# A gated transformer block on one core: SiLU products of batch 1 on VectorE, a fused variance, and another hand-set order

## The chip, the cores and the metric

The kernel runs on one core of a Trainium2 chip. The metric is the device time of one execution in microseconds, as the median of several runs. The profile is one execution; its times count from the first instruction.

## The reference

Four batches (B = 4) of 256 tokens with 128 features pass four sublayers, each with a residual scaled by the tanh of a gate:

```
x = x + tanh(g_xattn[0]) * L0_xattn(layernorm(x), ctx)      # autocorrelation attention over Fourier transforms, 16 heads
x = x + tanh(g_ffn[0])   * L0_ffn(layernorm(x))             # product-key memory, 8 heads, top 8 of 32 x 32 keys
x = x + tanh(g_xattn[1]) * L1_xattn(layernorm(x), ctx)      # attention with rotary positions, 16 heads of 8
x = x + tanh(g_ffn[1])   * L1_ffn(layernorm(x))             # 8 experts of 336 hidden units
```

In the product-key memory the queries `q = x @ w_q` (2048 columns) are normalised by their mean and variance over all tokens before they meet the keys:

```
mean, var = jnp.mean(q, axis=(0, 1)), jnp.var(q, axis=(0, 1))
q = (q - mean) * rsqrt(var + 1e-5) * gamma + beta
sim = einsum('pbnhd,hkpd->pbnhk', q, keys)        # then top 8 of each half, top 8 of the sums, softmax
h = softmax(scores) * gelu(x @ down_embed[indices]); out = h @ up_embed[indices]
```

Every expert of the last sublayer computes `y = (silu(x @ gate_w[e].T) * (x @ up_w[e].T)) @ down_w[e].T`, and the outputs are added with the router's probabilities, those past a token's own number of experts set to zero.

## The kernel before

Everything is float32 apart from one-hot and gathered operands in float16. The first sublayer, the layer norm behind it and the similarities run for all batches together, in the order of the code, up to about 96 us. **The variance** of the 2048 query columns comes from the covariance of the normalised input: TensorE makes `w_q.T @ cov` for 16 groups of 128 columns into six PSUM banks (`CW_BANK`), three groups a bank. VectorE copies the mean column, multiplies the bank by `w_qT` (L904) and, after a wait on its own product, sums it per column (L905). From the variance come the scaled keys `keyS` (L914), from them TensorE's product `M`, and from M the similarities (`similar`), tile by tile. Products with all down embeddings (`down_all`, 16 of them, for the GELU on ScalarE) are put in between; `EARLY` says how many of the first four ScalarE takes ahead of M, and three of them stand on TensorE ahead of M.

From there on each engine runs **a list of named steps written out by hand**, `ORDER` ("pe", "act", "dve", "pool"), a step being a name, a batch and a number: `gate2.7` is the eighth gate product of batch 2. An engine never passes a step whose semaphores are not yet there. Steps of the later text, in the order of one batch:

- retrieval: `best`, `where` (index search, L936), `pair`, `weight` (softmax and expert numbers, first line L978), `number`, `onehots`, `groups`, then for eight pieces of 32 tokens `place` (L1035, one-hot), `token` (TensorE), `half` and `weigh` (L1047, L1052), and `mix`, TensorE's product with the up embeddings; `norms1` adds it to x (L1060) and starts the next layer norm, whose root is on GpSimd (L439 to L446)
- attention: `turn_2`, `query`, `rope`, `turn_q`, four `by_query` with a maximum `max` each (L1097), `neg_max` (L1435 on TensorE), `score`, `prob`, `value`, `keep`, `out_turn`, `attend`, `project` (the product with Wo), `norms3` (again L1060 and GpSimd's root), `turn_3` (L1515)
- experts: 21 steps `gate` a batch, each 128 hidden units with the gate half and the up half in one of two PSUM banks; `silu` (L694), `times`, and for each expert a `down` on TensorE and a `gather` on VectorE (L1155, L1157), `moe_out` at the end; `route1`, `route2` and `rank` make the router's scores.

For batches outside `DIRECT`, ScalarE copies the up half to SBUF besides the SiLU, which frees the bank, and GpSimd multiplies the two (L433). For batches in `DIRECT` (2 and 3) VectorE multiplies the SiLU by the up half in PSUM (L1167), and that frees the bank: `gate` waits for it.

```
pe.wait_ge(sem("av_ready" if (m - 2) // NB in DIRECT else "gate_ready"), m - 1)
```

Of the kernel before, what the change touches and what calls it, by code (L numbers as in the profile page):

```python
# [66 lines left out]
gate0.2 by_query1.2 route20.0 token2.3 gate0.3 gate0.4 by_query1.3 token2.4 gate0.5 gate0.6 neg_max1.0 token2.5
gate0.7 score1.0 down0.0 token2.6 score1.1 value1.0 token2.7 score1.2 value1.1 mix2.0 score1.3 down0.1 onehots3.0
value1.2 gate0.8 gate0.9 value1.3 gate0.10 down0.2 turn_22.0 gate0.11 query2.0 gate0.12 out_turn1.0 turn_q2.0 token3.0
by_query2.0 down0.3 gate0.13 by_query2.1 attend1.0 token3.1 gate0.14 by_query2.2 gate0.15 token3.2 gate0.16 down0.4  # L70
by_query2.3 gate0.17 token3.3 gate0.18 project1.0 neg_max2.0 gate0.19 down0.5 token3.4 gate0.20 score2.0 down0.6
token3.5 turn_31.0 score2.1 value2.0 token3.6 gate1.0 score2.2 token3.7 route11.0 gate1.1 mix3.0 value2.1 gate1.2
route21.0 gate1.3 score2.3 down0.7 turn_23.0 gate1.4 value2.2 query3.0 gate1.5 down1.0 gate1.6 value2.3 gate1.7
turn_q3.0 down1.1 by_query3.0 gate1.8 out_turn2.0 gate1.9 by_query3.1 gate1.10 down1.2 gate1.11 down1.3 gate1.12
attend2.0 by_query3.2 gate1.13 project2.0 gate1.14 by_query3.3 gate1.15 down1.4 gate1.16 neg_max3.0 gate1.17 turn_32.0
gate1.18 gate1.19 score3.0 down1.5 gate1.20 down1.6 gate2.0 route12.0 gate2.1 route22.0 score3.1 down1.7 gate2.2
# [48 lines left out]
addb1.0 times0.11 times0.12 times0.13 times0.14 times0.15 times0.16 norms31.0 times0.17 times0.18 times0.19 times0.20  # L125
times1.0 times1.1 norms13.0 times1.2 times1.3 times1.4 times1.5 times1.6 addb2.0 times1.7 times1.8 times1.9 times1.10
times1.11 times1.12 times1.13 norms32.0 times1.14 times1.15 times1.16 times1.17 times1.18 addb3.0 times1.19 times1.20
norms33.0
# [1514 lines left out]
```

## Time and profile before

| quantity | value |
|---|---|
| median of 3 runs | 458.83 us (458.66 to 462.54) |
| the profiled execution's own time | 460.18 us |
| its span, first to last instruction | 458.3 us |
| mean granted TensorE clock | 0.881 |
| TensorE busy | 384.7 us (84%) |
| VectorE busy | 331.0 us (72%) |
| ScalarE busy | 197.4 us (43%) |
| GpSimd busy | 105.8 us (23%) |

Shares are averages over stages with different limits, so they say where to look and not what binds. The granted clock is the share of full speed that TensorE was given.

### The profile page before, as it was taken

How to read it: one execution, taken by the hardware profiler on the slowest of the kernel's cores; microseconds unless marked ns; L12 is line 12 of the kernel's file. 1: busy time of each engine (PE TensorE's matmuls, PEld its weight loads, DVE VectorE, ACT ScalarE, POOL GpSimd, SP SyncE). 2: the span in 40 equal slices, each digit the busy share in tenths (PEclk: the TensorE clock that was granted, in tenths of full speed). 3: DMA queues.
4: the chain of work that ended last, by engine and by line, in shares of the span. 5: the costliest groups of instructions: out<-in, count | busy, mean ns of one | idle time of the engine just before them, and what ended most of it. 6: DMA issues, size and time to landing. Idle time of an engine off the chain costs nothing.

```text
span 458.3 us, 8058 instructions
## 1 busy us (share of the span) xinstructions
PE 384.7 (84%) x2848; PEld 296.5 (65%) x2848; DVE 331.0 (72%) x1235; ACT 197.4 (43%) x399; POOL 105.8 (23%) x221
## 2 busy tenths in 40 slices
PE   8977699943462588995998899989999999999896
PEld 3856665412451366773787678866788886787785
DVE  7987674999999999989999888942444434354533
ACT  2453442551121011542486852366832698527221
POOL 2000020305047430073032381160432610010000
PEclk9989897985565575799599999988999999999999
DMA  7950000040000000000000000000000000000000
GB/s 228 332 224 0 1 1 2 1 153 8 1 1 1 1 1 0 1 2 1 1 2 1 1 2 2 0 1 2 12 2 0 1 1 14 1 0 1 13 0 11
DMA packets 5772, 11.80 MB, mean 26 GB/s; under 512 B 2020, under 2 KB 4325, under 8 KB 5222
## 3 DMA queue, kind: packets, MB, share of 16 engines
q1 hardware_dynamic: 5734, 11.31, 7.0%
q8 instruction: 22, 0.36, 0.3%
q14 instruction: 16, 0.13, 0.1%
HBM read 10.78 MB, written 0.52 MB: 25 GB/s over the span
## 4 chain that ended last, share of the span: by engine, by line
PE 37%; DVE 32%; issue 3%; ACT 3%; POOL 1%; DVEq 0%; ACTq 0%
PE ps L1193 35%; DVE mx L1097 5%; DVE Xb L1035 4%; DVE HDb L1052 3%; DVE tix L936 2%; DVE top L929 2%; DVE Y L1027 2%; PE ps L1435 1%; DVE pk L945 1%; DVE Xb L1047 1%; DVE xnb L1157 1%; ACT L564 1%; DVE Sb L1047 1%; DVE sb_downT L1017 1%; DVE hot L984 1%
## 5 line engine op out<-in xcount | busy, mean ns | idle before, releaser
L1193 PEld LDWEIGHTS ps<-dnb,Sb 128*128 128x128 f32 x448 | 54.2, 193 | 9.3 <-issue 3.9
L1193 PE MATMUL ps<-dnb,Sb 128*128 128x128 f32 x448 | 56.9, 279 | 3.8 <-POOL Sb L433 2.3
L1193 PE MATMUL ps<-Y,Xb 128*128 128x32 f16 x512 | 39.9, 250 | 15.8 <-DVE Xb L1035 10.6
L1193 PEld LDWEIGHTS ps<-Y,Xb 128*128 128x128 f16 x512 | 37.3, 162 | 23.1 <-DVE Xb L1035 17.1
L694 ACT ACTIVATE Sb<-ps 128x256 f32<-128x256 f32 x84 | 31.8, 382 | 37.4 <-PE ps L1193 37.4
L1157 DVE SCALAR_TENSOR_TENSOR xnb<-ps,score,xnb 128x128 f32<-128x128 f32 x56 | 17.0, 346 | 40.3 <-PE ps L1193 40.2
L1193 PE MATMUL ps<-ctxTb,sb_guT 128*128 128x256 f32 x168 | 45.5, 401 | 0.1
L1193 PE MATMUL ps<-Xb,sb_guT 128*128 128x256 f32 x168 | 43.7, 391 | 1.8 <-DVE Sb L1167 1.2
L471 ACT ACTIVATE Sb<-ps 128x256 f32<-128x256 f32 (+2 forms) x54 | 26.2, 492 | 35.8 <-PE ps L1193 20.0
L433 POOL TENSOR_TENSOR Sb<-Sb 128x256 f32<-128x256 f32 x28 | 21.7, 781 | 85.8 <-ACT Sb L694 85.8
L564 ACT ACT_TABLE_LOAD x32 | 41.1, 1283 | 0.6
L1035 DVE TENSOR_TENSOR Xb<-sb_downT,iox 128x2048 f16<-128x2048 f16 x32 | 39.6, 1248 | 1.7 <-PE ps L1193 1.3
L1097 DVE TENSOR_REDUCE mx<-ps 128x8 f32<-128x2048 f32 x16 | 36.6, 2286 | 3.8 <-PE ps L1193 3.7
L1167 DVE TENSOR_TENSOR Sb<-Sb,ps 128x256 f32<-128x256 f32 x42 | 17.4, 420 | 26.5 <-ACT Sb L694 26.2
L651 ACT ACTIVATE probs<-ps 128x1024 f32<-128x1024 f32 x32 | 31.2, 1020 | 9.2 <-PE ps L1193 9.1
L1193 PEld LDWEIGHTS ps<-Xb,sb_guT 128*128 128x128 f32 x168 | 29.1, 190 | 9.4 <-DVE Sb L1167 3.9
L1193 PEld LDWEIGHTS ps<-ctxTb,sb_guT 128*128 128x128 f32 x168 | 30.2, 197 | 7.3 <-issue 3.0
L1193 PE MATMUL ps<-KTb,Sb 32*128 32x256 f32 x256 | 21.3, 453 | 3.7 <-DVE mx L1097 3.5
L1193 PE MATMUL ps<-sb_upl,HDb 128*128 128x128 f32 x128 | 17.9, 306 | 4.6 <-DVE HDb L1052 4.6
L1193 PEld LDWEIGHTS ps<-sb_upl,HDb 128*128 128x128 f32 x128 | 17.1, 219 | 6.1 <-DVE HDb L1052 6.1
L936 DVE FIND_INDEX8 tix<-top,simb 128x8 uint32<-128x32 f32 x128 | 20.8, 185 | 0.0
L1193 PE MATMUL ps<-Sb,KTb 32*128 32x256 f32 x256 | 20.2, 434 | 0.1
(278 smaller groups left out, 707.0 us busy)
## 6 DMA issues: line engine op xcount, KB each, us to landing
sb_guT<-in_guT SPq DMA_DIRECT2D x1, 2688.0 KB
dnb<-in_dn SPq DMA_DIRECT2D x1, 1792.0 KB
simb<-in_w_q SPq DMA_DIRECT2D x1, 1024.0 KB, 4.9
simb<-in_w_qT SPq DMA_DIRECT2D x1, 1024.0 KB, 7.0
Gb<-in_ctx SPq DMA_DIRECT2D x1, 512.0 KB, 3.7
Gb<-in_dft SPq DMA_DIRECT2D x1, 512.0 KB, 4.5
sb_x<-in_x SPq DMA_DIRECT2D x1, 512.0 KB
sb_downT<-in_downT SPq DMA_DIRECT2D x1, 512.0 KB, 8.0
```

What stands on the lines that cost most here:

```text
L433: g.tensor_tensor(av[:, m % 6, :], av[:, m % 6, :], up[m % 3], ALU.mult).then_inc(sem("av_ready"), 1)
L471: act.activation(dst, src, ACT.Copy, scale=scale).then_inc(sem(s), 1)
L564: act.activation(sm[:, 63:64], tg[:, 0:1], func).then_inc(sem("table_ready"), 1)
L651: act.activation(probs[:, g % 2, 2 * half:2 * half + 2, :], ps[:, 4 + 2 * half:6 + 2 * half, :], ACT.Exp, scale=float(1.0 / np.sqrt(DK))). ...
L694: act.activation(av[:, m % 6, :], ps[:, m % 2, 0:256], ACT.Silu).then_inc(sem("gate_ready"), 1)
L936: i = v.max_index(tix[:, q, g, :], top[:, q, g, :], s3[:, g, :])
L1035: v.tensor_tensor(X[:, c % 2, :, :].rearrange("p (c e) t -> p c e t", c=EH), elS[:, :, c * TC:c * TC + TC].unsqueeze(2).broadcast_to([P, E ...
L1052: v.tensor_tensor(HD.rearrange("p e (s t) -> p s e t", s=2)[:, :, :, c * TC:c * TC + TC], w[:, :, :].rearrange("p s (t e) -> p s e t", e=E ...
L1097: v.tensor_reduce(mx[:, :, 4 * g:4 * g + 4].rearrange("p t r -> p r t"), ps[:, 4:8, :].rearrange("p r (t k) -> p r t k", t=2), AX, ALU.max)\
L1157: i = v.scalar_tensor_tensor(macc[:, t, :], y, w, macc[:, t, :], ALU.mult, ALU.add)
L1167: v.tensor_tensor(av[:, m % 6, :], av[:, m % 6, :], ps[:, m % 2, 256:512], ALU.mult).then_inc(sem("av_ready"), 1)
L1193: return pe.matmul(o, l, r, start=start, stop=stop)
```

## The change

Four things change. (1) The product and the sum of the variance become one fused instruction per group of 128 columns, with the sum as an accumulated output: 16 instructions instead of 6 products and 6 sums. (2) `EARLY` is 2 instead of 4: one `down_all` stands ahead of M instead of three, and the other three of the first four follow the first four `similar`; ScalarE takes their GELUs in the same order. (3) `DIRECT` gains batch 1: its 21 products leave GpSimd for VectorE, the 21 copies on ScalarE go, and its gates wait for VectorE's product. (4) All four lists of `ORDER` are written anew; batch 0 keeps its products on GpSimd.

```diff
@@ ORDER
-onehots0.0 token0.0 token0.1 token0.2 token0.3 token0.4 token0.5 token0.6 token0.7 mix0.0 onehots1.0 warm0.0 turn_20.0
...
+onehots0.0 token0.0 token0.1 token0.2 token0.3 token0.4 token0.5 token0.6 token0.7 mix0.0 onehots1.0 turn_20.0
...
@@ -305,9 +306,9 @@
             return 5 if b == 0 and c % 2 else 3
 
         G_BANK = [4 + n % 4 for n in range(2 * EH)]
-        EARLY = 4
+        EARLY = 2
         WARM = 3
-        DIRECT = (2, 3)
+        DIRECT = (1,2,3)
 
         block = ctx.enter_context(nc.Block())
 
@@ -588,8 +589,9 @@
             copy(M[:, :], ps[:, 7, :], "M_ready")
             similar(2)
             similar(3)
-            gelu(EARLY - 1)
-            for n in range(EARLY, EH):
+            for n in range(EARLY - 1, 4):
+                gelu(n)
+            for n in range(4, EH):
                 similar(n)
                 gelu(n)
             soft(0, 0)
@@ -901,8 +903,9 @@
                 cw = ps[:, bank, 0:m * (D + 1)].rearrange("p (c d) -> p c d", d=D + 1)
                 w = tmp[:, c0 * D:(c0 + m) * D].rearrange("p (c d) -> p c d", d=D)
                 v.tensor_copy(var[:, 2, c0:c0 + m], cw[:, :, D])
-                link(v.tensor_tensor(w, cw[:, :, 0:D], ld["w_qT"][:, c0:c0 + m, :], ALU.mult))
-                i = v.tensor_reduce(var[:, 3, c0:c0 + m], w, AX, ALU.add)
+                for c in range(m):
+                    i = v.scalar_tensor_tensor(w[:, c, :], cw[:, c, 0:D], 1.0, ld["w_qT"][:, c0 + c, :], ALU.mult, ALU.mult,
+                                               accum_out=var[:, 3, c0 + c:c0 + c + 1])
                 i.then_inc(sem("cw_used"), 1)
             v.wait_ge(sem("cw_used"), len(CW_BANK))
             link(v.tensor_tensor(var[:, 2, :], var[:, 2, :], var[:, 2, :], ALU.mult))
@@ -1342,7 +1345,7 @@
             for t in range(4):
                 shifted(t)
             pe.wait_ge(sem("xn1T_ready"), 1)
-            for n in range(3):
+            for n in range(EARLY - 1):
                 down_all(n)
             for c in range(16):
                 if c % 8 == 0:
@@ -1353,7 +1356,8 @@
             pe.wait_ge(sem("xcT_ready"), 1)
             for t in range(4):
                 similar(t)
-            down_all(3)
+            for n in range(EARLY - 1, 4):
+                down_all(n)
             for t in range(4, NT):
                 shifted(t)
                 similar(t)
```

**VectorE, before `norms3` of batch 0** (its three rows are the last of each list; L1108 and L1111 are the attention's divisions, sb_x is x). Before:

```order
L1108 RECIPROCAL rcp<-ps 128x32
L1109 TENSOR_TENSOR xnb<-ps,rcp 128x256
L1009 SCALAR_TENSOR_TENSOR whl<-ps,whl 128x128
L1014 TENSOR_TENSOR Xb<-elT,iox 128x1024
L1017 TENSOR_TENSOR sb_downT<-elT,sb_io 128x1024
L1027 TENSOR_TENSOR Y<-Xb,whl 64x1024 x4
L1060 SCALAR_TENSOR_TENSOR sb_x<-ps,tg,sb_x 128x256
L1065 BN_STATS st<-sb_x 128x6 x2
L1068 BN_AGGR mv<-st 128x2 x2
```

After (Xb is the one-hot of `place`, L788 to L793 the rope):

```order
L1111 RECIPROCAL rcp<-ps 128x32
L1112 TENSOR_TENSOR xnb<-ps,rcp 128x256
L1038 TENSOR_TENSOR Xb<-sb_downT,iox 128x2048 x2
L1095 MEMSET Sb 128x32
L788 TENSOR_TENSOR Sb<-ps,cs 128x256
L789 TENSOR_TENSOR Sb<-ps,cs 128x256
L792 TENSOR_TENSOR Sb<-Sb 128x32x4
L793 TENSOR_TENSOR Sb<-Sb 128x32x4
L1063 SCALAR_TENSOR_TENSOR sb_x<-ps,tg,sb_x 128x256
L1068 BN_STATS st<-sb_x 128x6 x2
L1071 BN_AGGR mv<-st 128x2 x2
```

Two `place` and the rope of batch 1 now stand between the divisions and `norms3`. Further up in the list the same holds of an index search, a `weight` and a `pair` of batch 3, ahead of that block:

```order
L939 MAX_INDEX tix<-top,simb 128x8 x16
L981 TENSOR_TENSOR hot<-pkf,iox 128x1280
L985 TENSOR_TENSOR hot<-hot,candi 128x1280
L987 TENSOR_TENSOR hot<-hot 128x640
L987 TENSOR_TENSOR hot<-hot 128x320
L988 TENSOR_REDUCE eid<-hot 128x64
L993 TENSOR_REDUCE zz<-ex_ 128x8
L994 RECIPROCAL zz<-zz 128x8
L995 TENSOR_TENSOR wts<-ex_,zz 128x8x8
L1063 SCALAR_TENSOR_TENSOR sb_x<-ps,tg,sb_x 128x256
L1068 BN_STATS st<-sb_x 128x6 x2
L1071 BN_AGGR mv<-st 128x2 x2
```

These are `where3.1` and `weight3.0`, and behind them `norms1` of batch 1; before, `where3.0` stood there directly in front of it.

**TensorE, from `project1.0` (sb_Wo) to `down0.6` (dnb, the last row).** Before:

```order
L1193 MATMUL ps<-sb_Wo,ctxTb 128x128 x2
L1435 MATMUL ps<-sb_ident,Sb 128x128 x8
L1193 MATMUL ps<-ctxTb,sb_guT 128x256 x2
L1193 MATMUL ps<-dnb,Sb 128x128 x6
L1193 MATMUL ps<-Y,Xb 128x2x16 x16
L1193 MATMUL ps<-ctxTb,sb_guT 128x256 x2
L1193 MATMUL ps<-Sb,KTb 128x256 x8
L1193 MATMUL ps<-dnb,Sb 128x128 x8
```

After:

```order
L1196 MATMUL ps<-sb_Wo,ctxTb 128x128 x2
L1196 MATMUL ps<-KTb,Sb 128x256 x8
L1196 MATMUL ps<-Y,Xb 128x2x16 x16
L1196 MATMUL ps<-dnb,Sb 128x128 x6
L1196 MATMUL ps<-ctxTb,sb_guT 128x256 x2
L1439 MATMUL ps<-sb_ident,Sb 128x128 x8
L1196 MATMUL ps<-Y,Xb 128x2x16 x16
L1196 MATMUL ps<-Sb,KTb 128x256 x8
L1196 MATMUL ps<-dnb,Sb 128x128 x8
```

A `by_query` (KTb) and a `token` (Y,Xb) have moved behind `project1.0`, and a `gate` (sb_guT) that stood ahead of `down0.6` stands behind it.

**VectorE among the first maxima of batch 3 (L1100; L1170 is the product with the up half, L1160 a `gather`).** After:

```order
L1158 TENSOR_SCALAR xnb<-ps,score 128x128 x2
L1170 TENSOR_TENSOR Sb<-Sb,ps 128x256
L1160 SCALAR_TENSOR_TENSOR xnb<-ps,score,xnb 128x128 x2
L1170 TENSOR_TENSOR Sb<-Sb,ps 128x256
L1100 TENSOR_REDUCE mx<-ps 128x4x2
L1160 SCALAR_TENSOR_TENSOR xnb<-ps,score,xnb 128x128 x2
L1170 TENSOR_TENSOR Sb<-Sb,ps 128x256 x3
L1100 TENSOR_REDUCE mx<-ps 128x4x2
L1170 TENSOR_TENSOR Sb<-Sb,ps 128x256
L1160 SCALAR_TENSOR_TENSOR xnb<-ps,score,xnb 128x128 x2
```

Before, these products were not on VectorE: between the maxima stood `gather` steps and the attention's divisions alone.

## Rows read from the trace of the kernel before

**Rows 1.** Stretches: busy us (instructions) of PE, PEld, DVE, ACT, POOL, clock, DMA, GB/s.
```profile
100.00:262.00 162.00, 114.77 (x1019) 90.03 (x1020) 154.09 (x624) 54.89 (x108) 51.51 (x119) 0.73 0.03 10
...
312.00:458.00 146.00, 138.37 (x1044) 112.67 (x1040) 62.86 (x183) 76.92 (x162) 22.76 (x47) 1.00 0.02 5
...
407.00:458.00 51.00, 45.09 (x280) 38.55 (x278) 22.42 (x71) 17.14 (x39) 1.53 (x6) 1.00 0.02 6
```

**Rows 2.** Timeline, 294 to 305 us: start, us, engine, instruction, [idle before, releaser].
```profile
294.64 0.61 PE L1193 MATMUL ps<-sb_Wo,ctxTb 128*128 128x128 f32 x4
...
297.68 0.23 POOL L439 TENSOR_SCALAR rs<-mv 128x2 f32<-128x2 f32 x1 [5.77 <-DVE mv L1068]
...
299.61 1.12 POOL L444 TENSOR_SCALAR rs<-rs 128x2 f32<-128x2 f32 x1
...
304.11 1.16 PE L1193 MATMUL ps<-dnb,Sb 128*128 128x128 f32 x8 [2.28 <-POOL Sb L433]
```

**Rows 3.** Stretches of 4 us behind that wait.
```profile
306.00:310.00 4.00, 4.00 (x38) 2.95 (x36) 2.36 (x5) 2.25 (x4) 0.00 (x0) 0.50 0.00 0
310.00:314.00 4.00, 4.00 (x40) 2.34 (x36) 0.71 (x2) 2.64 (x4) 0.00 (x0) 0.71 0.01 2
```

**Rows 4.** Timeline of VectorE in the variance, 54 to 70 us.
```profile
61.57 0.15 DVE L903 COPY var<-ps 128x3 f32<-128x3 f32 x1
...
62.69 0.15 DVE L903 COPY var<-ps 128x3 f32<-128x3 f32 x1
...
64.92 0.17 DVE L742 TENSOR_SCALAR var<-var 128x16 f32<-128x16 f32 x1
```

**Rows 5.** Timeline at 262 us, and the groups by form (busy us, mean ns).
```profile
262.72 0.61 DVE L1157 SCALAR_TENSOR_TENSOR xnb<-ps,score,xnb 128x128 f32<-128x128 f32 x2 [1.54 <-PE ps L1193]
...
L936 DVE MATCH_VALUE_LOAD tix<-top,simb 128x8 f32 x128 | 9.3, 72 | 0.1
```

**Rows 6.** Stretches of 1 us in M, TensorE alone: busy (matmuls), clock.
```profile
69.00:70.00 1.00, 1.00 (x11) 0.99 0.00 0
70.00:71.00 1.00, 1.00 (x7) 0.50 0.00 0
```

**Rows 7.** The chain that ended last: an index search of 16 pieces.
```profile
129.40 2.58 DVE tix L936 x16
```

**Rows 8.** Timeline, 247 to 263 us.
```profile
247.53 1.25 PE L1193 MATMUL ps<-Y,Xb 128*128 128x32 f16 x16 [1.16 <-DVE Sb L1047]
...
255.65 0.81 DVE L978 TENSOR_TENSOR hot<-pkf,iox 128x1280 f16<-128x1280 f16 x1
255.79 3.84 PE L1193 MATMUL ps<-sb_upl,HDb 128*128 128x128 f32 x32 [1.57 <-DVE HDb L1052]
...
259.90 0.48 DVE L1060 SCALAR_TENSOR_TENSOR sb_x<-ps,tg,sb_x 128x256 f32<-128x256 f32 x1
...
262.52 0.27 PE L1380 MATMUL ps<-sb_ident,elh 128*128 128x128 f32 x1
```

**Rows 9.** Groups of the page: busy us, mean ns, idle time before them.
```profile
L433 POOL TENSOR_TENSOR Sb<-Sb 128x256 f32<-128x256 f32 x28 | 21.7, 781 | 85.8 <-ACT Sb L694 85.8
...
L1035 DVE TENSOR_TENSOR Xb<-sb_downT,iox 128x2048 f16<-128x2048 f16 x32 | 39.6, 1248 | 1.7 <-PE ps L1193 1.3
L1097 DVE TENSOR_REDUCE mx<-ps 128x8 f32<-128x2048 f32 x16 | 36.6, 2286 | 3.8 <-PE ps L1193 3.7
L1167 DVE TENSOR_TENSOR Sb<-Sb,ps 128x256 f32<-128x256 f32 x42 | 17.4, 420 | 26.5 <-ACT Sb L694 26.2
```

**Rows 10.** Timeline, 203 to 221 us.
```profile
203.26 0.48 DVE L1060 SCALAR_TENSOR_TENSOR sb_x<-ps,tg,sb_x 128x256 f32<-128x256 f32 x1 [1.35 <-PE ps L1193]
...
212.62 0.48 DVE L1060 SCALAR_TENSOR_TENSOR sb_x<-ps,tg,sb_x 128x256 f32<-128x256 f32 x1
...
216.72 0.88 ACT L627 ACTIVATE xnb<-sb_x,nb,rs 128x128 f32<-128x128 f32 x2 [6.33 <-POOL nb L446]
...
220.55 0.66 PE L1515 MATMUL ps<-sb_ident,xnb 128*128 128x128 f32 x2
```

More of the change, by code:

```diff
@@ L67 @@
[L67 to L76, printed above, removed]
@@ new lines @@
+score1.0 down0.0 token2.5 score1.1 value1.0 token2.6 down0.1 token2.7 value1.1 score1.2 mix2.0 score1.3 down0.2
+onehots3.0 value1.2 gate0.8 gate0.9 value1.3 gate0.10 out_turn1.0 turn_22.0 gate0.11 query2.0 down0.3 gate0.12
+turn_q2.0 token3.0 gate0.13 by_query2.0 gate0.14 token3.1 attend1.0 gate0.15 by_query2.1 gate0.16 down0.4 by_query2.2
+gate0.17 token3.2 gate0.18 project1.0 by_query2.3 token3.3 down0.5 gate0.19 neg_max2.0 token3.4 score2.0 down0.6
+token3.5 gate0.20 score2.1 turn_31.0 token3.6 route11.0 gate1.0 token3.7 gate1.1 gate1.2 mix3.0 gate1.3 down0.7
@@ L107 @@
-pair3.0 attend0.0 groups2.0 norms30.0 where3.1 rope1.0 place2.0 pair3.1 place2.1 weigh2.0 place2.2 max1.0 place2.3
-weigh2.1 max1.1 place2.4 weigh2.2 max1.2 route20.0 weigh2.3 place2.5 max1.3 neg_max1.0 weigh2.4 rank0.0 place2.6
-weigh2.5 place2.7 gather0.0 weigh2.6 weight3.0 weigh2.7 weight3.1 norms12.0 gather0.1 groups3.0 gather0.2 place3.0
-rope2.0 place3.1 attend1.0 place3.2 max2.0 gather0.3 weigh3.0 max2.1 weigh3.1 place3.3 max2.2 weigh3.2 gather0.4
-place3.4 max2.3 neg_max2.0 weigh3.3 norms31.0 gather0.5 place3.5 weigh3.4 place3.6 gather0.6 weigh3.5 place3.7
@@ new lines @@
+weigh0.7 best2.0 weight1.1 where2.0 norms10.0 best2.1 groups1.0 where2.1 place1.0 pair2.0 rope0.0 place1.1 weight2.0
+weigh1.0 max0.0 place1.2 place1.3 weigh1.1 max0.1 weigh1.2 pair2.1 max0.2 place1.4 weigh1.3 max0.3 place1.5 neg_max0.0
+weigh1.4 place1.6 weight2.1 weigh1.5 place1.7 best3.0 weigh1.6 where3.0 best3.1 pair3.0 weigh1.7 where3.1 weight3.0
+norms11.0 pair3.1 groups2.0 attend0.0 place2.0 place2.1 rope1.0 norms30.0 weight3.1 place2.2 weigh2.0 max1.0 weigh2.1
+max1.1 place2.3 max1.2 weigh2.2 place2.4 max1.3 route20.0 neg_max1.0 weigh2.3 rank0.0 place2.5 weigh2.4 place2.6
@@ new lines @@
+gather0.0 weigh2.5 place2.7 weigh2.6 gather0.1 weigh2.7 norms12.0 gather0.2 groups3.0 attend1.0 place3.0 place3.1
+rope2.0 place3.2 gather0.3 weigh3.0 max2.0 weigh3.1 max2.1 place3.3 gather0.4 max2.2 weigh3.2 place3.4 norms31.0
+max2.3 neg_max2.0 weigh3.3 gather0.5 place3.5 weigh3.4 place3.6 gather0.6 place3.7 weigh3.5 weigh3.6 times1.0 weigh3.7
+times1.1 times1.2 norms13.0 gather0.7 times1.3 moe_out0.0 route21.0 rank1.0 times1.4 times1.5 rope3.0 gather1.0
+times1.6 gather1.1 times1.7 max3.0 gather1.2 times1.8 times1.9 times1.10 max3.1 times1.11 gather1.3 times1.12
@@ L124 @@
-times0.2 times0.3 times0.4 times0.5 look_a3.1 times0.6 number3.0 norms12.0 times0.7 times0.8 times0.9 times0.10
[L125 to L128, printed above, removed]
+look_a0.1 look_a1.0 cands1.0 cands1.1 gap1.0 look_a1.1 gap1.1 number1.0 look_a2.0 cands2.0 norms10.0 addb0.0 cands2.1
@@ L129 @@
+look_a2.1 gap2.0 gap2.1 cands3.0 number2.0 cands3.1 gap3.0 look_a3.0 look_a3.1 gap3.1 norms11.0 norms30.0 times0.0
+times0.1 times0.2 times0.3 times0.4 times0.5 times0.6 times0.7 number3.0 norms12.0 times0.8 times0.9 times0.10
+times0.11 times0.12 times0.13 times0.14 times0.15 times0.16 addb1.0 norms31.0 times0.17 times0.18 times0.19 addb2.0
+times0.20 norms13.0 norms32.0 addb3.0 norms33.0
 """,
```

81 lines of the change are left out of this document (41 added, 40 removed).

## The prediction

> **What bounds the kernel now.** I read the stretches first, then who waits for whom, then the timeline at the waits. The stretches [rows 1] give two regimes. From 100 to 262 us VectorE is busy 154.1 of 162 us: it does the key retrieval of all four batches and the attention maxima, and TensorE, busy 114.8 us at 0.73 of its clock, fits in between. Later TensorE is the bound: from 312 us on it is busy 138.4 of 146 us. So a VectorE microsecond taken away before 262 counts, one after it counts only if TensorE stands behind it; and behind 262 only TensorE's gaps and its half clock can be won. The largest such gap is one of 2.28 us at 301.8 us, where `down` of batch 0 waits for a multiplication on GpSimd; after it the clock reads 0.50 (1.2 GHz) for some microseconds [rows 2, 3]. Behind the last matmul a fixed tail of 3.4 us follows.
>
> **Part 1, the variance (58 to 71 us).** VectorE is on the path: TensorE waits for the scaled keys with which this work ends, and makes the product M from them. A group of three columns takes 1.12 us now, from one copy to the next (61.57 to 62.69) [rows 4]; the six take 5 x 1.12 + 0.7 = 6.3 us. The change makes three fused instructions per group, 16 in all, without the wait between product and sum. Its nearest row is a fused multiply-add from PSUM over 128x128: two of them take 0.61 us, so one starts some 0.27 us behind the other [rows 5]. No row has an accumulated output. If writing out the sum is free, a group costs 0.07 + 3 x 0.27 = 0.88 and all six 4.7 us (1.6 less); if it costs as much as a 16-element instruction, 0.17 [rows 4], a group costs 1.39 and all six 7.4 us (1.1 more). I take 0.07, the mean of the smallest instruction here, the value load of the index search [rows 5]: 1.09 a group, 5.8 us, 0.5 less. The Trainium skill (VectorE: DVE Perf Modes, section "Two Vector instructions with no wait between them") says that such an operation is two instructions, the main one and a read of the accumulator; it gives no time for the second, and no row here has one.
>
> With it goes EARLY 4 to 2: two `down_all` matmul pairs, 0.86 us each, are no longer ahead of M but behind the first four `similar`. In the trace they hide nothing that is missed: M starts on the keys (VectorE), and the GELUs have slack to 112 us. But TensorE now stands idle about 1.4 us before M, and its clock fell to 0.50 during M's narrow matmuls already (70 to 76 us), when it did 7 instead of 11 of them in a microsecond [rows 6]. Should it fall two microseconds sooner, M is about 1 us longer; if all of M runs so, 4.3 us become 6.7 (2.4 more). I take 0.5 more. Together part 1 is worth **0**, with ends at -1.6 and +2.4 (less of the one cancels the other).
>
> **Part 2, the new order up to the third mix (100 to 262 us).** VectorE's work is the same in total up to batch 2's residual, plus one `gather` of 0.61 us; it is in another sequence. Ahead of `norms3` of batch 0, the step that opens the mixture of experts, now stand `where3.1`, `weight3.0`, `pair3.1`, `place2.0`, `place2.1` and `rope1.0`: 2.6 + 4.2 + 2.0 + 2.5 + 1.2 = 12.5 us by their like in the trace: an index search of 16 pieces 2.58; a weight step from 255.65 to the next step's start at 259.90; a pair, with eight searches instead of sixteen and eight maxima, estimated at 2.0; 1.25 for each `place`; and a rope of four products, estimated from the 0.42 of a product of such a size [rows 7 to 9]. An idle spot goes, since something independent now stands in front of it: 1.35 us before the residual of batch 1; and some 0.3 of a smaller one before its divisions, in all 1.7 [rows 10]. So `norms3` starts at 212.6 + 12.5 - 1.7 = 223.4 us, and by the same 5.1 us through GpSimd and ScalarE the turn on TensorE (220.55 now, its input ready at 217.6) at 228.5: 8.0 us later [rows 10]. TensorE may not start a gate before it.
>
> Not all of this is lost, since in the stretch that follows VectorE has less left. Ahead of `weigh2.7` stand only `weight3.1` (4.1) and `gather0.1` (0.6) more than now, 4.7 us, less the 1.7: by VectorE the third `mix` starts 3.0 us later, at 258.8 instead of 255.79. By TensorE: from the turn to the mix it takes 35.2 us now, with 1.16 and 1.57 us of waits for VectorE [rows 8]; these go, `by_query1.0` (1.1) has moved ahead and `down0.1` (1.6) comes in: 33.0 us, so 261.5. The later one decides; with what remains of the half clock I take 261.1, which is +5.3 us. Against it stands `down0.1`, done already (1.6), and the transposition behind `down0.2`, which now waits for GpSimd's numbers until 262.5 and has them early then (0.5) [rows 8]. **+3.2**, ends +0.9 (VectorE alone decides) and +6.
>
> **Part 3, the gap at 301.8 us.** `project1.0` ends at 295.25; the residual and its statistics follow on VectorE, GpSimd's root from 297.68 to some 301.6, and only then the two multiplications that `down0.6` wants: TensorE goes on at 304.11 after 2.28 us [rows 2]. The clock is then 0.50 and 0.71 in two stretches of 4 us, 2.0 + 1.2 = 3.2 us of work [rows 3]. In the new order GpSimd's queue is the same at this place, `norms31` ahead of `times0.17`; the batch 1 multiplications that leave it stood behind. But TensorE has `by_query2.3` and `token3.3` between `project1.0` and `down0.6` and has lost `gate0.20`: 1.1 us each, so about 1.1 to 1.5 us more cover. The wait shrinks to about 0.8 us, the waits of 1.16 and 1.57 us before 247.53 and 255.79 us were followed by no such clock, and I count the half clock as won: **-4.8**. If all stays it is 0, if all goes -5.6.
>
> **Part 4, 21 multiplications to VectorE.** GpSimd loses 21 of some 0.78 us, ScalarE 21 copies, about 8 us if they cost what an activation of that size does, VectorE gains 21 of 0.42 us (8.8 us) [rows 9]; it is busy 62.9 of 146 us from 312 us on, so the work itself is covered. ScalarE's 8 us are not on the path either: only at 380 to 392 us does TensorE wait there. What is new is a wait: `gate1.n` on TensorE now needs the multiplication two before it, and that stands in VectorE's queue behind maxima of 2.29 us [rows 9], four of them, and the ranking, which I estimate at 3.5 us from its sixteen small steps of 0.17 to 0.3. Everything in TensorE's order queues behind the gate. The fourth batch has this wait on all its gates: TensorE is busy 45.1 of 51 us, and 3.4 of the rest are the tail, so 2.5 us for a batch, with a VectorE that has no maxima left [rows 1]. In the new order a `down`, `score` or `by_query` step stands between most pairs of gates. I take **+1.0**, ends 0 and +5.6 (one maximum and one ranking exposed).
>
> **Sum.** 0 + 3.2 - 4.8 + 1.0 = -0.6 us. The profiled run has a span of 458.3 us and a time of 460.18; the median of the runs shown is 458.83, and 1% (4.6 us) is about what a measurement of this kernel can tell from no change. I set the difference against the median: **458.2 us**, no change, its own range 454.5 to 462.5.
>
> **Rivals.** *Slower: VectorE's queue rules batch 1.* If the free steps between a gate and the multiplication it wants cover only about 1 us, each of four maxima shows 1.3 us and the ranking 2.3: 7.5 instead of 1.0, 464.7 us. For it: four maxima, the ranking and the rope lie among `times1.4` to `times1.17`. Against: VectorE is half idle there, and between the third maximum and the gate that follows TensorE has `down` and `value` steps of 1 to 2 us. It decides from about 2 us of exposed queue in half of the places.
> *Faster: VectorE alone decides at the mix.* Then the third mix starts at 258.8 (2.3 less), the gap at 301.8 goes whole (0.8), nothing is lost in batch 1 (1.0), and ScalarE without the copies shortens the waits of 380 to 392 us (1.2): 452.9 us. For it: the steps moved ahead fill real gaps. Against: TensorE has no slack from the turn on.
> *The gap stays.* A root of eight small GpSimd operations took 4.0 us from 297.68 on, one of them 1.12, while VectorE ran `place`; the one before 216.72, without it, took under 3 [rows 2, 10]; if it is held up as long again, 0.8 becomes 2.3 with the half clock: 463.0 us. The Trainium skill (GPSIMD Engine Reference, "1. Specifications") says that GpSimd's SBUF interfaces are shared with VectorE, in contention with its two-port modes and with two SBUF inputs; by that rule, the trace agrees, and such a hold would come wherever `place` stands beside the root.
> *The fused variance brings nothing* (accumulator read 0.17): +1.6 on any case.
>
> **Chances.** Forecast 0.38, faster rival 0.28, slower 0.22, gap stays 0.12. 452.9 with its spread lies mostly, the forecast's low end partly under 454.2: faster 0.31; 464.7 mostly and 463.0 for a third above 463.4, with the forecast's high end 0.25; same 0.44. The range takes in the middles of both outer rivals: 451 to 465.5.
>
> **What would show it.** The variance: six groups in less than 6.3 us. Part 2: the first gate at 228 to 230 us, the third mix at 259 to 262. Part 3: no GpSimd wait over 1 us in front of `down0.6` and a clock of 1.00 behind it. Part 4: TensorE's waits for the multiplication line sum to under 4 us in batch 1. I would be wrong if the maxima wait for TensorE in a chain (VectorE idle over 10 us before 262 us), which none of these terms has.

## The result

The changed kernel takes **462.67 us** (median of 8 runs, 462.31 to 464.07); the kernel before takes 458.63 us beside it (8 runs). The ratio is 1.0068, 95% interval [1.0038, 1.0098]: 0.7% slower, small and outside the measurement's uncertainty. The forecast was 458.2. In a later session the same comparison gave 1.0051 [1.0016, 1.0087]. The profiled execution has a span of 461.5 us, a time of 463.25 and a granted clock of 0.885.

I take the steps in the order of time. **The variance**, as VectorE's timeline shows it (start, us, instruction):

```profile
57.43 0.16 DVE L905 COPY var<-ps 128x3 f32<-128x3 f32 x1 [4.32 <-PE ps L1196]
57.51 0.28 DVE L907 SCALAR_TENSOR_TENSOR Gb<-ps,simb 128x128 f32<-128x128 f32 x1
57.71 0.08 DVE L907 DVE_READ_ACCUMULATOR Gb<-ps,simb 128x1 f32 x1
57.71 0.29 DVE L907 SCALAR_TENSOR_TENSOR Gb<-ps,simb 128x128 f32<-128x128 f32 x1
...
58.13 0.16 DVE L905 COPY var<-ps 128x3 f32<-128x3 f32 x1
...
63.33 0.76 DVE L917 TENSOR_TENSOR Gb<-Gb,var 128x256 f32<-128x256 f32 x2
...
70.42 0.69 DVE L922 COPY simb<-ps 128x512 f32<-128x512 f32 x1 [6.33 <-PE ps L1196]
```

A group of three takes 58.13 - 57.43 = 0.70 us, where it was 1.12 [rows 4]: fused instructions start 0.20 to 0.21 us apart, and the accumulator's read is a record of its own of 0.08 us that lies under the next one. The keys are scaled 5.90 us behind the first copy (8.30 before), and the first similarities leave PSUM 12.99 us behind it (15.91 before). I count from the first copy, since its own place varies from 57.4 to 60.6 us between the profiled executions, whatever the kernel.

**The turn of batch 0 into the experts.** The timeline from 209 us on, where GpSimd, ScalarE, TensorE and VectorE hand over to one another:

```profile
209.72 2.00 POOL L414 TENSOR_TENSOR dd<-sc 128x64 f32<-128x64 f32 x1 [4.03 <-DVE pk L948]
...
211.67 0.95 POOL L417 CAST pkf<-pk 128x64 f16<-128x64 uint32 x1
212.35 0.72 POOL L440 TENSOR_SCALAR rs<-mv 128x2 f32<-128x2 f32 x1
...
217.91 0.20 POOL L447 TENSOR_TENSOR nb<-rs 128x2 f32<-128x2 f32 x1
218.14 0.88 ACT L629 ACTIVATE xnb<-sb_x,nb,rs 128x128 f32<-128x128 f32 x2 [9.14 <-POOL nb L447]
219.07 0.69 PE L1422 MATMUL ps<-sb_ident,xnb 128*128 128x128 f32 x2 [7.98 <-ACT xnb L629]
...
223.34 0.39 DVE L788 TENSOR_TENSOR Sb<-ps,cs 128x256 f32<-128x256 f32 x1 [5.84 <-issue]
...
224.50 0.48 DVE L1063 SCALAR_TENSOR_TENSOR sb_x<-ps,tg,sb_x 128x256 f32<-128x256 f32 x1
...
231.87 0.33 PE L1519 MATMUL ps<-sb_ident,xnb 128*128 128x128 f32 x1 [1.29 <-ACT xnb L629]
```

L414 and L417 are `gap3.1`; L440 to L447 are the root of batch 1's layer norm (`norms11.0`), L1422 its turn, L788 the rope that needs this batch's queries, L1063 `norms3` of batch 0 and L1519 its turn. The statistics of that layer norm were there at about 207.7 us; the root begins at 212.35, because GpSimd stands at `gap3.1`, whose input comes from VectorE's `pair3.1`. TensorE then waits 7.98 us, VectorE 5.84 us in front of the rope. The turn is at 231.87, where it was 220.55 [rows 10].

**Behind the turn.** The stretches of the page's columns (PE, PEld, DVE, ACT, POOL busy, clock), and TensorE's timeline:

```profile
100.00:232.00 132.00, 76.83 (x653) 60.59 (x654) 122.01 (x540) 26.17 (x53) 50.24 (x107) 0.65 0.01 5
...
306.00:310.00 4.00, 3.93 (x49) 3.43 (x47) 3.93 (x7) 3.69 (x7) 3.47 (x4) 1.00 0.02 4
310.00:314.00 4.00, 4.00 (x48) 3.26 (x47) 3.69 (x6) 2.48 (x4) 0.00 (x0) 1.00 0.00 0
```

```profile
265.00 1.27 PE L1196 MATMUL ps<-sb_upl,HDb 128*128 128x128 f32 x9
...
428.66 1.13 PE L1196 MATMUL ps<-Xb,sb_guT 128*128 128x256 f32 x4 [1.21 <-DVE Sb L1170]
...
456.24 1.58 PE L1196 MATMUL ps<-dnb,Sb 128*128 128x128 f32 x12 [0.79 <-DVE xnb L1160]
```

The third `mix` starts at 265.00 without a wait (255.79 and 1.57 us of wait before [rows 8]). From its start to the end of the last matmul, 457.82, it is 192.8 us; before it was 198.9. The wait for GpSimd at `down0.6` is gone, and so is the half clock behind it (0.50 and 0.71 in [rows 3], 1.00 now). So the change gains in the variance and in the tail, and loses more in between: from 100 to 262 us VectorE stands idle for 14.9 us, where it was 7.9.

### The profile page after: what moved, and what is told of

The parts are those of the page before. It is cut to its first block, busy times and chain, and to the rows that moved or that the text cites. A ratio compares the mean times of both kernels' runs of the same rounds, so it can differ in the third digit from the quotient of the medians.

```text
span 461.5 us, 8058 instructions
## 1 busy us (share of the span) xinstructions
PE 378.7 (82%) x2848; PEld 293.9 (64%) x2848; DVE 334.8 (73%) x1276; ACT 192.9 (42%) x378; POOL 95.5 (21%) x200
## 4 chain that ended last, share of the span: by engine, by line
PE 40%; DVE 5%; ACT 4%; issue 3%; POOL 1%; DVEq 0%; ACTq 0%
PE ps L1196 38%; ACT L565 2%; PE ps L1439 1%; ACT probs L653 1%; DVE Xb L1038 1%; DVE Sb L1170 1%; ACT Sb L696 1%; DVE Y L1030 1%; DVE mx L1100 0%; POOL Sb L434 0%; DVE xnb L1160 0%; ACT Sb L472 0%; POOL nb L447 0%; PE ps L1519 0%; DVE sb_downT L1020 0%
## 5 line engine op out<-in xcount | busy, mean ns | idle before, releaser
L1170 DVE TENSOR_TENSOR Sb<-Sb,ps 128x256 f32<-128x256 f32 x63 | 25.9, 419 | 39.0 <-ACT Sb L696 37.0
L1100 DVE TENSOR_REDUCE mx<-ps 128x8 f32<-128x2048 f32 x16 | 36.6, 2286 | 3.0 <-PE ps L1196 2.8
L1196 PEld LDWEIGHTS ps<-Xb,sb_guT 128*128 128x128 f32 x168 | 29.1, 190 | 10.2 <-DVE Sb L1170 6.2
L472 ACT ACTIVATE Sb<-ps 128x256 f32<-128x256 f32 (+2 forms) x40 | 21.1, 534 | 31.1 <-PE ps L1196 18.0
L1160 DVE SCALAR_TENSOR_TENSOR xnb<-ps,score,xnb 128x128 f32<-128x128 f32 x56 | 17.0, 345 | 21.2 <-PE ps L1196 21.1
L440 POOL TENSOR_SCALAR rs<-mv 128x2 f32<-128x2 f32 x8 | 2.9, 358 | 100.1 <-DVE mv L1071 100.1
L1196 PE MATMUL ps<-KTb,Sb 32*128 32x256 f32 x256 | 19.0, 412 | 2.8 <-DVE mx L1100 2.8
```

The source lines that it names most:

```text
L472: act.activation(dst, src, ACT.Copy, scale=scale).then_inc(sem(s), 1)
L1100: v.tensor_reduce(mx[:, :, 4 * g:4 * g + 4].rearrange("p t r -> p r t"), ps[:, 4:8, :].rearrange("p r (t k) -> p r t k", t=2), AX, ALU.max)\
L1160: i = v.scalar_tensor_tensor(macc[:, t, :], y, w, macc[:, t, :], ALU.mult, ALU.add)
L1170: v.tensor_tensor(av[:, m % 6, :], av[:, m % 6, :], ps[:, m % 2, 256:512], ALU.mult).then_inc(sem("av_ready"), 1)
L1196: return pe.matmul(o, l, r, start=start, stop=stop)
```

## The experiments

First all of them in one table. "Copy to similar" is from VectorE's first variance copy to its first copy of the similarities, "to mix 2" to TensorE's second `mix`, "to the turn" to the turn of batch 0 (L1519 of the changed kernel), "to the end" to the end of the last matmul; all in us, of the profiled execution.

| run | median, us | ratio to before, 95% | copy to similar | to mix 2 | to the turn | to the end |
|---|---|---|---|---|---|---|
| before | 458.63 | | 15.9 | 141.2 | 162.3 | 396.4 |
| after | 462.67 | 1.0068 [1.0038, 1.0098] | 13.0 | 142.7 | 174.4 | 400.4 |
| changed_again | 462.65 | 1.0051 [1.0016, 1.0087] | 13.1 | 142.6 | 174.4 | 400.3 |
| root_first | 456.60 | 0.9947 [0.9911, 0.9984] | 12.4 | 140.7 | 168.0 | 392.9 |
| norms30_first | 457.80 | 0.9956 [0.9932, 0.9980] | 12.7 | 142.4 | 170.3 | 393.8 |
| direct_off | 460.30 | 0.9990 [0.9952, 1.0028] | 12.4 | 140.6 | 167.9 | 396.7 |
| part1 | 457.16 | 0.9955 [0.9921, 0.9990] | 12.5 | 138.1 | 159.3 | 390.8 |
| fused_only | 457.83 | 0.9966 [0.9930, 1.0003] | 15.5 | 141.2 | 162.4 | 393.8 |
| early_only | 460.42 | 0.9978 [0.9939, 1.0017] | 18.2 | 145.1 | 166.3 | 397.3 |
| early_again, one run | 457.13 | | 15.4 | 140.9 | 162.0 | 393.5 |
| head_before | 457.61 | 0.9956 [0.9921, 0.9991] | 12.4 | 138.6 | 159.9 | 392.7 |
| part1_times | 459.51 | 0.9964 [0.9923, 1.0004] | 12.4 | 138.8 | 160.0 | 397.8 |
| part1_times_again, one run | 459.55 | | 13.1 | 138.1 | 159.3 | 395.8 |

The kernel before had medians of 459.31 (root_first, part1, fused_only, head_before), 460.15 (direct_off, part1_times, early_only, changed_again) and 459.95 us (the rest) in the three later sessions, so ratios are compared, not medians across sessions. The column "to mix 2" is there because after, changed_again, root_first, norms30_first and direct_off have the same steps on every engine up to that point, so what differs there is not their edit.

### root_first: the root ahead of gap3.1

```diff
@@ ORDER "pool" of the changed kernel
-look_a3.1 gap3.1 norms11.0 norms30.0
+look_a3.1 norms11.0 gap3.1 norms30.0
```

> The changed kernel with one pair swapped in GpSimd's list: norms11.0 (the root of batch 1's layer norm) ahead of gap3.1 instead of behind it. In the changed kernel the root starts at 212.35 us, 4.7 us after its input, because gap3.1 waits for a VectorE step that comes later, and VectorE then stands idle for 5.84 us before the rope of batch 1. Theory (GpSimd's queue delays the front): the root runs from about 207.8 us, the idle before the rope falls from 5.84 to under 2 us, the turn of batch 0 on TensorE comes 3 to 5 us earlier than 231.87, and as TensorE is busy without a gap from there, the time falls by 3 to 5 us, to 457.5 to 459.5. Rival (the VectorE steps moved ahead of norms3 delay it, and the idle only shifts): less than 1 us, 461.5 to 462.7.

Its timeline at the same place:

```profile
206.53 0.22 POOL L440 TENSOR_SCALAR rs<-mv 128x2 f32<-128x2 f32 x1 [2.07 <-DVE mv L1071]
...
208.49 1.88 POOL L445 TENSOR_SCALAR rs<-rs 128x2 f32<-128x2 f32 x1
...
211.17 0.62 POOL L447 TENSOR_TENSOR nb<-rs 128x2 f32<-128x2 f32 x1
211.75 0.29 POOL L414 TENSOR_TENSOR dd<-sc 128x64 f32<-128x64 f32 x1
...
212.76 0.69 PE L1422 MATMUL ps<-sb_ident,xnb 128*128 128x128 f32 x2 [2.91 <-ACT xnb L629]
...
217.61 0.39 DVE L788 TENSOR_TENSOR Sb<-ps,cs 128x256 f32<-128x256 f32 x1 [1.21 <-issue]
...
226.14 0.44 PE L1519 MATMUL ps<-sb_ident,xnb 128*128 128x128 f32 x2 [1.01 <-ACT xnb L629]
```

The idle time ahead of the rope falls from 5.84 to 1.21 us, the turn comes 6.5 us earlier behind the first copy, and the kernel is 1.2 points faster than the changed one (0.9947 against 1.0068; the two intervals do not meet). Of the 6.5 us, 2.0 are there at the second `mix` already, ahead of the moved step, and are not its doing (TensorE's clock behind M, below). Counted from the second mix, the turn comes 4.5 us earlier and the last matmul 5.5 (the clock from the turn to the third mix reads 0.95 here and 0.90 there). One word in the list of the least busy engine was worth some 5 us. **changed_again** rules out that the chip made it:

> The changed kernel once more, unchanged, in the same session as the others, since the sessions differ by up to 1 us. Theory: 0.5 to 1% above the kernel before, 5 to 7 us above root_first's 456.6; the root of batch 1's layer norm starts 4 to 6 us later than in root_first, after a gap3.1 operation of about 2 us. Rival (the chip of the first session made the difference, not GpSimd's order): within 2 us of root_first's distance to the kernel before.

It gave 1.0051 and the same distances within 0.2 us. The first theory held.

### part1, fused_only, early_only, early_again: the variance taken apart

All four keep the order and the GpSimd products of the kernel before. part1 has the fused variance and `EARLY = 2`, fused_only the fused variance with `EARLY = 4`, early_only the old product and sum with `EARLY = 2`; early_again is early_only once more.

```diff
-        EARLY = 4
+        EARLY = 2          # part1, early_only, early_again
-                link(v.tensor_tensor(w, cw[:, :, 0:D], ...))     # part1, fused_only
-                i = v.tensor_reduce(var[:, 3, c0:c0 + m], w, AX, ALU.add)
+                    i = v.scalar_tensor_tensor(w[:, c, :], ..., accum_out=var[:, 3, c0 + c:c0 + c + 1])
```

> The kernel before with the fused variance and EARLY = 2 alone: its own order, batch 1 on GpSimd. In the changed kernel the first similarity tile was copied 3.7 us earlier (70.42 against 74.11). Theory (VectorE is the bound up to 262 us, so it passes on): 3.0 to 3.8 us faster than before, 454.9 to 455.7. Rival (M and the clock took it by chance in one execution, or it is lost in a wait of the retrieval): less than 1.5 us faster, 457.2 to 458.7. If the prediction's sizes held (0.5 for the fused step, nothing for EARLY): 458.1.

> The kernel before with the fused variance alone, EARLY = 4 as before. Between the first copy and the scaled keys the changed kernel took 5.90 us against 8.30, 2.4 less. If the fused step alone makes the gain: 2.4 us faster than before and within 0.5 of the run with both. If EARLY = 2 holds the clock up during M or frees the start of M: up to 1.3 us less of a gain than that run. With EARLY = 4 two more matmul pairs of 0.86 us stand ahead of M, and the keys now come 2.4 us sooner, so M should wait for these matmuls: I expect 1.0 to 2.0 us less gain than with both, that is 0.7 to 2.4 us faster than before.

> The kernel before with EARLY 2 instead of 4 and the variance in its two old steps. Theory (the fused variance and EARLY work together: with EARLY 4 the fused one only waits, with EARLY 2 alone the keys are still late): from the first variance copy to the first copy of sim 15.0 to 15.9 us, against 15.9 before, 15.5 with the fused variance alone and 12.5 with both; time within 1 us of the kernel before. Rival (EARLY alone does it, because the two pairs held M back and let the clock fall): 13.5 us or less and 2 us or more faster than before.

> early_only a second time, one look, since one profile can't tell whether the half clock in M belongs to the kernel. Theory (M behind an idle spot of 1.7 us falls to half clock): M's 32 narrow matmuls and their two copies take 6.5 us or more again, granted clock 0.50 from 68 us on, first variance copy to first copy of sim 17.5 us or more. Rival (chance of one execution): clock 1.00 in M, 15 to 16 us.

From first copy to similarities, against 15.9 before: both parts 12.5, the fused variance alone 15.5, `EARLY` alone 15.4 (early_again). So neither does much alone and both together 3.4 us. By the medians the three can't be told apart: 0.9955 with both, 0.9966 and 0.9978 with one, intervals overlapping. So part1, 2.1 us faster than the kernel before by its ratio, falls between its two expectations, and fused_only, 1.6 us faster, inside its own. TensorE's timeline in fused_only shows one half of the reason:

```profile
63.46 2.74 PE L1195 MATMUL ps<-dnb,sb_downT 128*128 128x512 f32 x6
66.03 1.20 PE L1195 MATMUL ps<-Gb,simb 128*128 128x32 f32 x10
```

The keys are ready at about 64 us, and M starts at 66.03, behind six matmuls (`down_all`), of which `EARLY = 2` leaves two. With `EARLY = 2` and the old variance it is the other way round: TensorE is free and the keys come late. So M starts 8.6 and 8.8 us behind the first copy with one part, 8.8 before, and 6.9 with both (part1, root_first). My prediction looked at the two edits one at a time, and the profile of before already had the warning:

```profile
64.27 2.74 PE L1193 MATMUL ps<-dnb,sb_downT 128*128 128x512 f32 x6
```

These six matmuls end as M starts (66.98), so earlier keys alone had next to nothing to win.

The other half is the clock behind M. Stretches of TensorE (busy, matmuls, clock) in fused_only, and then in root_first:

```profile
70.00:72.00 2.00, 1.31 (x3) 0.50 0.00 0
72.00:74.00 2.00, 2.00 (x4) 0.50 0.00 0
```

```profile
70.00:72.00 2.00, 2.00 (x6) 1.00 0.00 0
72.00:74.00 2.00, 2.00 (x6) 1.00 0.03 8
```

All four profiles that lack one or both parts read 0.50 from M's last matmuls on (early_only from its first), for some 6.8 us in three of them, the kernel before among them, and 10.2 in early_only. Of the nine profiles with both parts, five read it for some 3.4 us (after, changed_again, norms30_first, part1, part1_times_again) and four not at all (root_first, direct_off, head_before, part1_times). So in these profiles the two edits together shortened the half clock. Which of the two a profile with both parts shows is chance, and with it goes a difference of 1.7 to 2.0 us at the second mix among the five kernels that have the same steps up to there.

early_only has a second lesson. Stretches of TensorE in M (busy, matmuls, clock), first of early_only:

```profile
68.00:70.00 2.00, 2.00 (x11) 0.50 0.00 0
70.00:72.00 2.00, 2.00 (x11) 0.50 0.00 0
```

and of early_again, the same kernel:

```profile
68.00:70.00 2.00, 2.00 (x20) 1.00 0.00 0
70.00:72.00 2.00, 1.31 (x7) 0.62 0.00 0
```

11 against 20 matmuls in 2 us, 18.2 against 15.4 us to the similarities: M ran at 1.2 GHz in one execution and at 2.4 GHz in the other, behind the same idle spot of 1.70 us (behind M both read 0.50). Of early_only I had expected 15.0 to 15.9, and by its first profile that missed; of the repeat I had expected the half clock in M to return, and it didn't. Here the rival (chance of one execution) held.

part1 is as fast as root_first: 0.9955 against 0.9947. So everything beyond Part 1 in the change, with its one misplaced word mended, brings nothing that these runs can tell from zero.

### norms30_first: the residual ahead of the rope

```diff
@@ ORDER "dve" of root_first
-place2.0 place2.1 rope1.0 norms30.0
+place2.0 place2.1 norms30.0 rope1.0
```

> This is root_first with norms3 of batch 0 ahead of the rope of batch 1 on VectorE, instead of behind it. Theory (what stands ahead of that residual is on the path of the turn, one for one): the residual starts about 1.1 us earlier after the two place steps, the turn 0.7 to 1.1 us earlier, and the last matmul at most 1 us earlier, about 456 us where the kernel before takes 459. Rival (TensorE then waits for the rope instead: turn_q1 and by_query1.0 stand ahead of turn_30 and queue behind it): the turn does not move or comes later, 456.5 to 458 us.

The rival held. The timeline of VectorE and TensorE:

```profile
221.85 0.48 DVE L1063 SCALAR_TENSOR_TENSOR sb_x<-ps,tg,sb_x 128x256 f32<-128x256 f32 x1 [2.32 <-PE ps L1196]
...
224.49 0.71 PE L1196 MATMUL ps<-Y,Xb 128*128 128x32 f16 x8 [2.67 <-DVE Sb L793]
```

VectorE now waits 2.32 us for `project0.0`, which TensorE reaches only behind `query1.0`, and TensorE waits 2.67 us for the rope. Behind the first copy the turn is 2.3 us later than in root_first and the end 0.9 us, but 1.7 of that is there at the second mix, where the lists are still the same (the clock behind M). From the second mix the turn is 0.6 us later. The last matmul is 0.8 us earlier, but from the turn to the third mix the clock reads 1.00 instead of 0.95 and TensorE is busy 1.5 us less with the same steps, so the end shows no gain; from that mix on both take 192.8 us. The ratios, 0.9956 and 0.9947, can't tell the two apart.

### head_before: the old order up to the third mix

The lists of before up to `norms12.0` (VectorE, GpSimd) and `onehots3.0` (TensorE, ScalarE), those of the changed kernel behind them; `DIRECT` with batch 1, the variance as changed.

> The changed kernel with the lists of the kernel before up to the third mix (to norms12, onehots3 and their like on each engine) and its own lists from there; fused variance, EARLY = 2 and batch 1 on VectorE stay. Theory (the new order up to the mix costs, the one behind it gains): the front gives back 3.7 us of the early part and the mix starts at about 252 us; from there on to the end it takes 196 to 198 us instead of 202.5: 449 to 452 us. Rival (the tail's gain depends on the front, for instance because work was only moved between them): the tail takes 200 to 202 us, 453 to 456.

The turn comes 8.1 us earlier than in root_first and the third `mix` 5.2 us, both counted from the first copy (194.9 against 200.1 us), yet the last matmul ends at the same distance (392.7 and 392.9 us). The tail is 197.8 us long here and 192.8 in root_first. Two of these 5.0 us are work: TensorE is busy 189.3 us of it against 187.3, since `down0.1`, done before the mix in the new order, is done behind it here. The other three are waits, the larger one where the two orders meet, for products that stand behind the root of batch 2 on GpSimd:

```profile
263.07 1.60 PE L1195 MATMUL ps<-dnb,Sb 128*128 128x128 f32 x12 [2.57 <-POOL Sb L433]
265.54 1.07 PE L1195 MATMUL ps<-probs,V 128*32 128x256 f32 x16 [0.86 <-DVE xnb L1159]
```

The rival, a tail whose gain depends on the front, held: from the mix to the end of the span it is 201.4 us. The median of 457.61 us lies above the ranges of both.

### direct_off: batch 1's products back on GpSimd

```diff
-        DIRECT = (1,2,3)
+        DIRECT = (2, 3)
@@ ORDER "dve" of root_first: times1.0 to times1.20 taken out
@@ ORDER "pool" of root_first: from times0.17 on as in the kernel before
```

> This is root_first (the changed kernel with batch 1's root ahead of gap3.1 on GpSimd) with the 21 multiplications of batch 1 back on GpSimd and ScalarE's copies, in the places that they had in the kernel before. Theory (part 4 costs little and brings little, since TensorE is the bound there): within 1.5 us of root_first's distance to the kernel before, so about 456 to 458 us in a session where the kernel before takes 459; TensorE's waits from 305 us on sum to within 1 us of root_first's. Rival (the multiplications on VectorE are what makes the tail 6 us shorter): turn_30 to the last matmul takes 228 us or more, against 224.9 in root_first, and the time is 3 us or more above root_first's.

Longer than root_first by 2.7 us from the third mix on and by 3.8 us from copy to end, by the ratios 0.4 points. The 1.1 us between the two numbers are there at the third mix, ahead of the edit (a clock of 0.90 instead of 0.95 from the turn on), so 2.7 us are the edit's. TensorE and GpSimd in its timeline:

```profile
358.09 0.22 POOL L440 TENSOR_SCALAR rs<-mv 128x2 f32<-128x2 f32 x1 [6.43 <-DVE mv L1071]
...
360.56 0.19 POOL L447 TENSOR_TENSOR nb<-rs 128x2 f32<-128x2 f32 x1
360.70 0.72 POOL L434 TENSOR_TENSOR Sb<-Sb,Xb 128x256 f32<-128x256 f32 x1
361.39 1.41 POOL L434 TENSOR_TENSOR Sb<-Sb 128x256 f32<-128x256 f32 x2
...
362.17 1.05 PE L1196 MATMUL ps<-dnb,Sb 128*128 128x128 f32 x7 [2.50 <-POOL Sb L434]
```

The pattern of [rows 2] again, one batch later: a root of 2.7 us on GpSimd stands ahead of the products that a `down` wants. This is what Part 4 removes in the new order. Between my two expectations (within 1.5 us of root_first; 3 us or more above it with a tail over 228 us behind the turn) the result lies between them: 228.8 us behind the turn, but 227.7 without the 1.1 us that are not the edit's, and 0.4 points by the medians, whose intervals overlap.

### part1_times: the products ahead of the root at 301 us

```diff
@@ ORDER "pool" of part1
-times0.16 norms31.0 times0.17 times0.18
+times0.16 times0.17 times0.18 norms31.0
```

> This is part1 (the kernel before with the fused variance and EARLY 2) with GpSimd's times0.17 and times0.18 ahead of the root of batch 1's second norm, so that down0.6 on TensorE does not stand behind that root. Theory (the wait of about 2.3 us on GpSimd in front of down0.6 is a real loss of the path): that wait is gone, 1.5 to 2.3 us less than part1, about 455 us. Rival (TensorE takes the time back at the next wait, for the third mix or for turn_31, whose root is now later by two multiplications of 0.95 us): the wait is gone, the last matmul ends within 0.7 us of part1's, about 457 us.

> part1_times a second time, one look, since its profiled execution was 4 us above its own median. Theory (the wait moves from GpSimd to ScalarE, where the exponentials of batch 2 queue behind the normalisation that needs the later root): TensorE waits 3 us or more for ScalarE's probs at about 306 us again. Whether the half clock of 308 to 317 us follows again is open; with it about 463, without it about 459 us.

GpSimd's wait is gone and nothing is won: 0.9964 against part1's 0.9955. The first profiled execution took 463.88 us against a median of 459.51, so it alone proves little; the second took 459.55, and both show the same wait. GpSimd, ScalarE and TensorE in the first:

```profile
304.99 0.19 POOL L446 TENSOR_TENSOR nb<-rs 128x2 f32<-128x2 f32 x1
...
305.22 0.89 ACT L628 ACTIVATE xnb<-sb_x,nb,rs 128x128 f32<-128x128 f32 x2 [3.46 <-POOL nb L446]
...
308.07 1.92 ACT L652 ACTIVATE probs<-ps 128x1024 f32<-128x1024 f32 x2
...
310.04 2.09 PE L1195 MATMUL ps<-Sb,KTb 32*128 32x256 f32 x16 [3.43 <-ACT probs L652]
```

Counted from the third mix the root ends 2.4 us later than in part1 (2.7 in the second execution), ScalarE waits for it with the exponentials of batch 2 queued behind, and TensorE waits 3.43 us for those instead of 2.3 us for GpSimd. My expectation (2 us faster) failed; the rival (the wait gone, the time unchanged) holds by the medians. By the profiles it was too kind: from the third mix to the last matmul it is 199.9 us in the second and 201.4 in the first, where part1 has 196.5. (The rest of the 5 and 7 us by which the end is later than in part1 is there at the third mix, ahead of the edit: the clock from the turn to the mix reads 0.83 and 0.82 instead of 0.91.) The clock read 0.50 from within this wait on in both (309 to 318 us in the first, 306 to 312 in the second).

## Why the prediction was wrong

**Part 2 failed**, at the step "`norms3` starts at 212.6 + 12.5 - 1.7 = 223.4 us". It summed VectorE's work ahead of `norms3` and took VectorE as never waiting. It measured 224.50, which looks like a hit and is two errors: with Part 1's gain of about 3 us it should have been 220.5 at the latest, and it was so in root_first (218.77, its first copy 0.75 us later, 2.0 us of it by the clock behind M). The missing term is the 5.84 us that VectorE stood idle in front of the rope. The rope was in my list, priced with four products and with no look at its input: layer norm, turn, query of batch 1, whose root GpSimd reached only after `gap3.1`. I had compared GpSimd's list at `times0.17` alone. And "the same 5.1 us through GpSimd and ScalarE" was 7.4 (224.50 to 231.87), since this root too ran beside VectorE's products, 5.0 us (225.88 to 230.91) instead of under 3. From the turn to the mix the estimate held: 33.1 us, predicted 33.0. With the root in its place, the mix stands 2.5 us later than before behind the first copy, or 6.0 without Part 1's 3.5; predicted +5.3. In the changed kernel it is 10.0 us later, or 12.9 without Part 1's 2.9: an error of 7.6 us, and the reason for the sign. The sign that I had set for being wrong, VectorE idle over 10 us before 262, came (14.9 us), but not for the reason given: the maxima waited for TensorE once, 2.0 us, and the largest wait was the 5.84 us in front of the rope.

**Part 1 was mis-sized**: 0 predicted, ends at -1.6 and +2.4, measured -2.9 to the first similarities, outside both. A group costs 0.70 instead of 1.09: the fused instruction starts each 0.21 us, not 0.27 + 0.07, because the read does not delay the next product. The other half is `EARLY`: I priced it at +0.5 (clock), and it is what lets M use the earlier keys. The clock term had the wrong sign: the half clock of 6.8 us that the kernel before has behind M became 3.4 us or none. In M itself the feared half clock was seen once (early_only).

**Parts 3 and 4 came out near their sum, in part by luck.** Behind the mix I had -1.6 - 0.5 - 4.8 + 1.0 = -5.9; measured 192.8 - 198.9 = -6.1. GpSimd's wait of 2.28 us and the half clock did vanish. But the half clock does not belong to that wait: part1, fused_only, early_only and early_again all keep the wait at `down0.6` of 2.3 us and run at 1.00 behind it, as part1 shows (TensorE's timeline, and the stretch behind it):

```profile
303.28 0.94 PE L1195 MATMUL ps<-dnb,Sb 128*128 128x128 f32 x6 [2.29 <-POOL Sb L433]
```

```profile
308.00:312.00 4.00, 4.00 (x53) 1.00 0.03 6
```

So some 2.4 of the 4.8 us were the chance of one execution, which itself took 1.35 us more than the median (460.18 against 458.83), and I set a difference that contained them against the median. (The terms of Part 3 add up to 1.5 + 3.2 = 4.7, not 4.8.) Part 4's cost of +1.0 did not come: TensorE never waits for a product of batch 1, whose gates run from 315.6 to 369.9 us. Its two waits for the product line from 305 us on, 0.34 us at 378 and 1.21 at 428.66, belong to batches 2 and 3, which had 1.9 us of them before. In the new order Part 4 has a gain that I had not seen, the root of batch 2 out of the products' way (2.50 us in direct_off; the kernel before has no wait at that root). That the sum fits is in part luck: the wait that was to remain (0.8) and Part 4's cost (1.0) were both too dear, and smaller losses elsewhere, such as a wait of 0.71 us for ScalarE at 383 us, made up for them.

Of the rivals "the gap stays" (463.0) came nearest in time and was wrong in place: at `down0.6` there is no wait and no half clock. Its mechanism, a root on GpSimd that is held up beside VectorE, did come, at the norms of batch 1 and batch 0 further up. The slower rival (464.7, VectorE's queue in batch 1) fell, with no such wait in batch 1. The faster rival fell at the mix, which TensorE decides, as the forecast said. "The fused variance brings nothing" fell. That the chain would wait for GpSimd in front of `norms3` was in none of the cases.

**Why the mended order is not better than part1**, although its tail from the third mix on is 3.7 us shorter (192.8 against 196.5): its turn comes 8.7 us later behind the first copy (168.0 against 159.3), it makes up 2.9 from the turn to the mix (at a clock of 0.95 against 0.91) and 3.7 behind it, and ends 2.1 us later. Of the 3.7, 1.8 are work moved ahead of the mix (TensorE busy 187.3 against 189.0 us) and 1.9 are waits saved. By the ratios (0.9947 and 0.9955) the two are equal.

**What stays open:** whether the steps behind the mix can be had without the later turn. head_before was to show it and has a wait of its own where the orders meet. Nor was the root placed elsewhere than on GpSimd.

## What to carry over

When a list of steps is rewritten, follow each moved step's inputs back through every engine's list, the idlest engine's above all: a queue that is 21% busy can hold the path through one item that waits. Price two edits at one hand-over together, since each alone may only lengthen a wait. Before a difference between two profiles is put down to an edit, look whether it is there ahead of the edit: 2.0 of the 6.5 us of root_first were. And take a half clock behind a wait as a property of the kernel only if a second execution shows it; otherwise leave it out of the sum.
